# Normalising the last head group in the transposed layout: 0/1 selection matrices in column tiles instead of transposes, and one joint second variance

## Chip, cores and metric

One core of one Trainium2 chip runs the whole kernel. The metric is the device time of one execution in microseconds, the median of the runs. All data is float32 (the scores use float32r).

## What is computed

One transformer layer over 2048 tokens of 128 values, 16 heads of 8:

```python
def kernel_func(q, k):                      # attention weights without softmax
    scores = einsum('bhqd,bhkd->bhqk', q, k) / sqrt(HD)
    w = relu(scores)
    return w / (sum(w, axis=-1, keepdims=True) + 1e-6)
xn  = layernorm(x)
out = (kernel_func(q, k) @ v) @ w_out + b_out          # q, k, v from xn @ w_qkv
y   = xn + out
x1  = x + (y - mean(y)) * rsqrt(var(y) + 1e-5) * gamma + beta
h   = layernorm(x1)
x2  = x1 + sqrt((h @ cos(theta + theta_noise))**2 + (h @ sin(phi + phi_noise))**2)
```

## The kernel before

The engines' programs are written by hand, each with its own order of instructions; semaphores join them. The queries are cut into NC = 4 chunks of CW = 512 columns, the heads into G = 4 groups of HPG = 4. A pass takes one chunk through 4 x 16 steps: a step computes the scores of 128 keys for the four heads of a group in four row tiles of the array (`score_step`, L1119), ScalarE and VectorE share the relu (L603, L609, L781, L786), and `value_step` (L1154) multiplies by the values in four column tiles, one head in each 32 rows of a PSUM bank `pv`. The 32 rows of a head hold its 8 value rows, then at row HD = 8 the sum of the weights, then zeros. ScalarE copies the finished bank to `pv_sb`.

For passes 0 to 2 the normalisation goes through DRAM and is spread over the following pass: SyncE saves `pv_sb`, loads the sums and the values in other layouts, VectorE adds the epsilon and inverts (`invert_sums`), SyncE spreads the inverses, GpSimd multiplies (`scale_o`) into `oT` (heads x 8 rows, tokens along the columns), the stationary operand of the projection. The hooks in `after_pass` say at which step each engine does its part. The epsilon of each token is scaled by its standard deviation (`eps_std`); transposed, it lies in DRAM as `eps_dram`, from which four loads fill `eps_spread` at the end of pass 0.

The last chunk has no pass behind it. Its first three groups go the same way through DRAM during the last group (96 rows of `oT`). The last group, rows 96 to 128, is the tail, done in two halves of 256 tokens:

- ScalarE copies each half of `pv[1]` to `pv_sb` (L693).
- TensorE transposes it, tokens onto partitions (`transpose_pv`, L1161); VectorE adds the epsilon, inverts, multiplies (`normalise`, L796, L800, L801) into `o_sb`, whose other columns are zero; TensorE transposes back (`transpose_o`, L1161); ScalarE copies the 32 rows to `oT` (`take_oT`, L635).
- TensorE adds the projection to the residual in PSUM: `tail_x` (L1257) multiplies x_tail by the identity to start a bank, `project_tail` (L1267) adds the projection. Each half has two such banks: which = 0 for the statistics, which = 1, scaled by gamma, for x1.
- VectorE takes mean and variance (L950, L956), ScalarE the root (L696), VectorE inverts it (L962) and makes x1 (`tail_x1`, L969).
- TensorE transposes x1 (`transpose_x1`), ScalarE copies it (L644), TensorE multiplies by the centred cos and sin (`ffn`, L1212), ScalarE squares (L649), VectorE adds the squares (`tail_sum`, L979), ScalarE takes the root scaled by the second variance (`magnitude`, L659), VectorE adds x1 (`tail_finish`, L987), SyncE stores. The second variance comes from `post_stats` and `post_inverse` on x1 (L857 to L867), one half after the other.

Of the kernel before, what the change touches and what calls it, by code (L numbers as in the profile page):

```python
# [58 lines left out]
NORM_SEQ = 2  # L59
# [21 lines left out]
def block_kernel(nc, x, w_qkv, w_out, b_out, gamma, beta, theta, phi, theta_noise, phi_noise, out):  # L81
# [3 lines left out]
    with ctx:  # L85
        def sb(name, shape, dt=F32):
            return ctx.enter_context(nc.sbuf_tensor(name, shape, dt))

        def sem(name):
            return ctx.enter_context(nc.semaphore(name))  # L90
# [25 lines left out]
        den = sb("den", [P, TPC, HPG])  # L116
# [6 lines left out]
        o_sb = sb("o_sb", [P, TPC, D])  # L123
# [8 lines left out]
        turns = sb("turns", [P, 2, D])  # L132
        ffn_w = sb("ffn_w", [P, 2, D])
# [87 lines left out]
        pvT_done = sem("pvT_done")  # L221
# [8 lines left out]
        o_zero = sem("o_zero")  # L230
        norm_own = sem("norm_own")
        normed = sem("normed")

        oT_done = sem("oT_done")
# [32 lines left out]
        def chunk(c):  # L267
            return bass.ds(c * TPC, TPC)

        class Part:  # L270
# [3 lines left out]
            def __init__(self, j, half=None):  # L274
                self.j, self.half = j, half
                self.n = j if half is None else j + half
                self.lo, self.tiles = (0, TPC) if half is None else (2 * half, 2)
                self.own = (post_own[half or 0], POST_SEQ * (0 if half else j))
                if half is None:
                    self.o_bank = self.y_bank = pv[1]  # L280
                    self.x1_bank = pv[0]
                else:
                    self.pv_bank, self.o_bank = sc[half][:, 0, :], sc[half][:, 1, :]
                    self.y_bank = sc[2][:, half, :]
                    self.x1_bank = self.pv_bank
# [38 lines left out]
        with nc.Block() as block:  # L324

            @block.sync
            def _(sp):
# [103 lines left out]
            def _(pool):  # L431
# [41 lines left out]
                nc.gpsimd.memset(o_sb[:, :, 0:(G - 1) * HPG * HD], 0.0).then_inc(o_zero, 1)  # L473
# [61 lines left out]
                nc.gpsimd.memset(eps_col[:, :], LN_EPS).then_inc(eps_ready, 1)  # L535
                scale_o(0, G)
# [15 lines left out]
            def _(act):  # L552
# [79 lines left out]
                def take_oT(part):  # L632
                    last = slice((G - 1) * HPG * HD, P)
                    act.wait_ge(oT_done, part.half + 1)
                    nc.scalar.copy(oT[last, part.cols()],  # L635
                                   part.o_bank[last, 0:part.tiles * P]).then_inc(oT_ready, 1)

# [65 lines left out]
                for stage in (square, magnitude):  # L703
                    for part in halves:
                        stage(part, 0)
                        stage(part, 1)
# [3 lines left out]
            def _(dve):  # L710
# [78 lines left out]
                def normalise(half, bank, tiles):  # L789

                    own = Own(dve, norm_own, NORM_SEQ * half)
                    n = tiles.stop - tiles.start
                    pvT = bank[:, 0:n * P].rearrange("p (t i v) -> p t i v", t=n, i=HPG)
                    dve.wait_ge(pvT_done, half + 1)
                    first_tile = (NC - 1) * TPC
                    own(nc.vector.tensor_tensor(  # L796
                        den[:, tiles, :], pvT[:, :, :, HD],
                        eps_std[:, first_tile + tiles.start:first_tile + tiles.stop].unsqueeze(2).to_broadcast(
                            [P, n, HPG]), ALU.add))
                    own(nc.vector.reciprocal(den[:, tiles, :], den[:, tiles, :]))  # L800
                    nc.vector.tensor_tensor(  # L801
                        o_sb[:, tiles, (G - 1) * HPG * HD:].rearrange("p t (i d) -> p t i d", i=HPG),
                        pvT[:, :, :, 0:HD], den[:, tiles, :].unsqueeze(3).to_broadcast([P, n, HPG, HD]),
                        ALU.mult).then_inc(normed, 1)

                def invert_sums(c, groups):
# [6 lines left out]
                    dve.wait_ge(eps_loaded, 16 * NC)  # L813
# [174 lines left out]

                for part in halves:
                    normalise(part.half, part.pv_bank, part.sl())  # L990
# [3 lines left out]
                tail_stats(second)  # L994
                tail_inverse(first)
                tail_variance(second)
# [3 lines left out]
                for stage in (lambda p: post_stats(p, x1), lambda p: post_inverse(p, 1)):  # L1000
                    for part in halves:
                        stage(part)
                dve.wait_ge(x2_ready, NC - 1)
                for stage in (tail_sum, tail_finish):
                    for part in halves:
                        stage(part, 0)
                        stage(part, 1)
# [3 lines left out]
            def _(pe):  # L1011
# [152 lines left out]
                def transpose_pv(half, bank, tiles):  # L1164
                    pe.wait_ge(pv_out, G * NC + half)
                    transpose_tiles(bank, lambda t: pv_sb[:, t * P:(t + 1) * P], tiles, pvT_done)

                def transpose_o(part):
                    pe.wait_ge(o_zero, 1)
                    pe.wait_ge(normed, part.half + 1)  # L1170
                    transpose_tiles(part.o_bank, lambda t: o_sb[:, t, :], part.all(), oT_done)
# [99 lines left out]
                pe.wait_ge(tail_ready, 2)  # L1271
                tail_x(first, 1, pv[0])
                for part in halves:
# [37 lines left out]
```

## Time and profile before

| | |
|---|---|
| three runs | 421.67, 421.72, 548.05 us (median 421.72) |
| profiled execution | 422.16 us, of which the span from first to last instruction is 420.4 |
| busy: TensorE, VectorE, ScalarE, GpSimd | 98%, 79%, 81%, 12% of the span |
| granted TensorE clock | 1.00 in all of the span |
| last value matmul ends | 407.05 us after the span's start |

All times are from the start of the span. Busy shares are means over passes (TensorE always at work) and a tail (nobody is); the tail is read from the timelines.

### The profile page before, as it was taken

Reading aid. Unit: us, or ns where it says so; the run is one execution under the profiler, and the core shown is the slowest. Engines: PE = TensorE matmul, PEld = TensorE weight load, DVE = VectorE, ACT = ScalarE, POOL = GpSimd, SP = SyncE. Lnnn points to the kernel's source line nnn. Section 1 sums busy time; section 2 is a strip of 40 time slices with the busy share of each in tenths; the row PEclk is TensorE's granted clock in tenths of the full one; section 3 lists DMA queues with packets and bytes.
Section 4 is the critical chain, followed back from the end, with each engine's and each line's share of the span. In section 5 each row is a group of like instructions: output and inputs, shape, how many; then the busy total and the mean of one; then the engine's idle time right before and its main releaser. Section 6 shows DMA issues by size and latency. Waiting matters only on the chain.

```text
span 420.4 us, 8994 instructions
## 1 busy us (share of the span) xinstructions
PE 412.1 (98%) x3263; PEld 120.0 (29%) x3263; DVE 331.6 (79%) x654; ACT 341.1 (81%) x611; POOL 49.4 (12%) x57
## 2 busy tenths in 40 slices
PE   8899999999999999999999999999999999999995
PEld 6333222222222222222222322222222322222234
DVE  5877778888688897777778898777778798777856
ACT  3879888888788888888888888788887888888864
POOL 2004000099101000000401000000100100000111
PEclk9999999999999999999999999999999999999999
DMA  5117841010021100001011100101012000000200
GB/s 168 31 51 147 162 114 51 2 27 25 4 75 46 51 2 21 33 0 52 27 53 55 27 27 8 43 2 52 27 50 58 2 27 1 27 2 27 68 2 25
DMA packets 11741, 17.54 MB, mean 42 GB/s; under 512 B 3684, under 2 KB 5364, under 8 KB 11316
## 3 DMA queue, kind: packets, MB, share of 16 engines
q1 hardware_dynamic: 11556, 16.84, 15.0%
q8 instruction: 28, 0.46, 0.4%
q10 hardware_dynamic: 144, 0.13, 0.1%
q14 instruction: 13, 0.11, 0.1%
HBM read 3.99 MB, written 5.11 MB: 22 GB/s over the span
## 4 chain that ended last, share of the span: by engine, by line
PE 97%; DVE 2%; ACT 1%; issue 0%; POOL 0%; POOLq 0%; DVEq 0%
PE pv L1154 61%; PE sc L1119 27%; PE pv L1212 2%; PE pv L1054 1%; PE pv L1074 1%; PE pv L1066 1%; PE pv L1045 1%; PE pv L1180 1%; PE pv L1161 0%; PE pv L1034 0%; PE sc L1212 0%; PE sc L1081 0%; DVE x L969 0%; PE sc L1161 0%; PE sc L1267 0%
## 5 line engine op out<-in xcount | busy, mean ns | idle before, releaser
L1154 PE MATMUL pv<-w_buf,v_sb 128*32 128x512 f32 x2048 | 272.3, 604 | 0.0
L781 DVE TENSOR_SCALAR w_buf<-sc 128x512 f32<-128x512 f32 x256 | 176.9, 691 | 68.9 <-PE sc L1119 59.2
L603 ACT ACTIVATE w_buf<-sc 128x512 f32<-128x512 f32 x256 | 153.2, 598 | 62.8 <-PE sc L1119 61.5
L609 ACT ACTIVATE w_buf<-sc 128x512 f32<-128x512 f32 (+1 forms) x254 | 182.5, 719 | 0.0
L1119 PE MATMUL sc<-q_rep,k_rep 32*128 32x512 f32 x1024 | 133.2, 494 | 1.0 <-DVE w_buf L781 0.9
L786 DVE TENSOR_SCALAR w_buf<-sc 128x512 f32<-128x512 f32 x182 | 125.0, 687 | 0.0
L1119 PEld LDWEIGHTS sc<-q_rep,k_rep 32*128 32x128 f32 x1024 | 52.0, 181 | 215.0 <-ACT w_buf L603 176.5
L1154 PEld LDWEIGHTS pv<-w_buf,v_sb 128*32 128x32 f32 x2048 | 40.4, 108 | 66.5 <-ACT w_buf L609 35.4
L494 POOL TENSOR_TENSOR oT<-o_raw,o_scale 128x512 f32<-128x512 f32 (+1 forms) x4 | 5.1, 1281 | 88.4 <-issue 60.8
L510 POOL TENSOR_TENSOR mag<-sq 128x256 f32<-128x256 f32 x6 | 4.4, 731 | 77.5 <-ACT sq L649 77.5
L500 POOL TENSOR_TENSOR x<-x,mv 128x512 f32<-128x512 f32 (+1 forms) x5 | 4.3, 870 | 68.2 <-DVE x L883 55.7
L514 POOL TENSOR_TENSOR x<-x,mag 128x512 f32<-128x512 f32 x3 | 3.8, 1280 | 52.7 <-ACT mag L659 52.7
L453 POOL TENSOR_TENSOR xn<-x_sb,mv 128x512 f32<-128x512 f32 x4 | 4.2, 1043 | 42.8 <-issue 42.8
L444 POOL MEMSET v_sb<- 128x1472 f32 x4 | 5.2, 1326 | 31.6 <-DVE inv_var L736 31.6
L617 ACT COPY pv_sb<-pv 128x512 f32<-128x512 f32 x15 | 8.8, 586 | 0.1
L1212 PE MATMUL pv<-ffn_w,x1T 128*128 128x256 f32 x24 | 6.8, 405 | 0.0
L742 DVE TENSOR_TENSOR q_lo<-pv,q_hi 128x512 fp32r<-128x512 f32 x4 | 2.8, 692 | 4.0 <-ACT q_hi L568 4.0
L659 ACT ACTIVATE mag<-mag,iv_p 128x128 f32<-128x128 f32 x16 | 5.4, 398 | 0.0
L484 POOL TENSOR_TENSOR x_sb<-x_sb,beta_b 128x512 f32<-128x512 f32 x4 | 5.0, 1271 | 0.0
L1074 PE MATMUL pv<-ident 128*128 128x128 f32 x14 | 3.4, 432 | 1.5 <-POOL ident L434 1.5
L1212 PEld LDWEIGHTS pv<-ffn_w,x1T 128*128 128x128 f32 x24 | 4.1, 189 | 1.8 <-issue 1.5
L1045 PE MATMUL pv<-xT,w 128*128 128x512 f32 x8 | 4.4, 637 | 0.1
(132 smaller groups left out, 152.3 us busy)
## 6 DMA issues: line engine op xcount, KB each, us to landing
pv_dram<-pv_sb SPq DMA_DIRECT2D x15, 256.0 KB, 2.0
q_rep<-q_hi SPq DMA_DIRECT2D x30, 64.0 KB, 2.1
q_rep<-q_lo SPq DMA_DIRECT2D x30, 64.0 KB, 2.1
k_rep<-k_hi SPq DMA_DIRECT2D x6, 256.0 KB, 4.1
k_rep<-k_lo SPq DMA_DIRECT2D x6, 256.0 KB, 5.4
x_sb<-x_dram SPq DMA_DIRECT2D x3, 256.0 KB, 3.9
o_raw<-pv_dram SPq DMA_DIRECT2D x3, 256.0 KB
o_scale<-inverse_dram SPq DMA_DIRECT2D x3, 256.0 KB
```

The costliest lines, as they stand in the source:

```text
L444: nc.gpsimd.memset(v_sb[:, :, heads, HD + 1:VW], 0.0).then_inc(v_pad, 1)
L603: nc.scalar.activation(w_buf[:, s % W_STEPS, 0, :], early[:, 0, :], ACT.Relu).then_inc(relu[0], 2 if none else 1)
L609: nc.scalar.activation(w_buf[:, s % W_STEPS, 2:2 + n, :], late[:, 0:n, :], ACT.Relu).then_inc(relu[0], 1)
L617: nc.scalar.copy(pv_sb[:, :], bank[:, :]).then_inc(pv_out, 1)
L659: last = nc.scalar.activation(mag[:, t, :], mag[:, t, :], ACT.Sqrt, scale=iv_p[:, 1, t:t + 1])
L781: nc.vector.tensor_scalar(w_buf[:, s % W_STEPS, 1, :], early[:, 1, :], 0.0, None, ALU.max).then_inc(relu[1], 2 if both else 1)
L786: nc.vector.tensor_scalar(w_buf[:, s % W_STEPS, 2 + n:4, :], late[:, n:2, :], 0.0, None, ALU.max).then_inc(relu[1], 1)
L1045: nc.tensor.matmul(k_bank[c], w3[:, 1, :], xT[:, c * CW:(c + 1) * CW], start=True, stop=True).then_inc(k_done, 1)
L1074: nc.tensor.matmul(bank[:, 0:P], ident[:, :], ident[:, :], start=True, stop=True)
L1119: last = nc.tensor.matmul(sc[buf][:, i % 2, :], k_rep[rows, g, k * P:(k + 1) * P], q_rep[rows, g, :], start=True, stop=True)
L1154: last = nc.tensor.matmul(bank[32 * i:32 * i + 32, :], v_sb[:, k, HPG * g + i, :], w_buf[:, s % W_STEPS, i, :], start=(k == 0), stop=(k == ...
L1212: last = nc.tensor.matmul(bank[:, m * 2 * D:(m + 1) * 2 * D], x1T[:, t * P:(t + 1) * P], ffn_w[:, :, :].rearrange("p c d -> p (c d)"), sta ...
```

## The change

- The epsilons of the last chunk are loaded once more, by SyncE at the end of pass 0, as `eps_tail`: the row of 512 tokens on all 128 partitions.
- GpSimd makes two 128x32 matrices of zeros and ones from the identity (`select`, in the space of `turns`): `select[:, 0, :]` brings a head's sum row to the 8 rows of this head, `select[:, 1, :]` its 8 value rows to them.
- In place of the transposes TensorE runs `start_sums` (identity columns times `eps_tail` start the sum's rows of a bank with the epsilon) and `select_rows` (sums and values), each into 32 rows of a bank: one column tile.
- VectorE's `normalise` inverts 32 rows x 256 columns from PSUM into `o_scale`, and multiplies the values by it straight into `oT`. `o_sb`, `den`, `transpose_pv`, `transpose_o` and `take_oT` go.
- `tail_x(first, 1)` moves from in front of the tail to behind the second projection. The second half's `tail_variance` moves ahead of the first half's inverse.
- The second variance is made once for both halves (`x1_inverses`). ScalarE's squares and roots interleave.

```diff
+                            sp.dma_start(eps_tail[:, :], eps_dram[chunk(NC - 1), :].rearrange("t p -> (t p)")
+                                         .partition_broadcast(P)).then_inc(eps_loaded, 16)
...
-                nc.gpsimd.memset(o_sb[:, :, 0:(G - 1) * HPG * HD], 0.0).then_inc(o_zero, 1)
...
+                by_head = ident[:, :].rearrange("p (i v) -> p i v", i=HPG)
+                for n, columns in enumerate((by_head[:, :, HD:HD + 1].to_broadcast([P, HPG, HD]),
+                                             by_head[:, :, 0:HD])):
+                    nc.gpsimd.tensor_copy(select[:, n, :].rearrange("p (i d) -> p i d", i=HPG),
+                                          columns).then_inc(tail_ready, 1)
...
-                for stage in (take_oT, tail_root, take_x1T):
+                for stage in (tail_root, take_x1T):
                     for part in halves:
                         stage(part)
...
+                first, second = halves
+                square(first, 0)
+                square(first, 1)
+                square(second, 0)
+                magnitude(first, 0)
+                square(second, 1)
+                magnitude(first, 1)
+                magnitude(second, 0)
+                magnitude(second, 1)
...
+                def normalise(part):
+
+                    rows, cols = slice((G - 1) * HPG * HD, P), part.cols()
+                    dve.wait_ge(den_done, part.half + 1)
+                    if part.half == 0:
+                        dve.wait_ge(oT_ready, NC - 1)
+                    nc.vector.reciprocal(o_scale[rows, cols],
+                                         part.den_bank[part.den_rows, 0:part.tiles * P]).then_inc(den_inverse, 1)
+                    dve.wait_ge(den_inverse, part.half + 1)
+                    nc.vector.tensor_tensor(oT[rows, cols], part.o_bank[part.o_rows, 0:part.tiles * P],
+                                            o_scale[rows, cols], ALU.mult).then_inc(oT_ready, 1)
...
-                    dve.wait_ge(eps_loaded, 16 * NC)
+                    dve.wait_ge(eps_loaded, 16 * (NC + 1))
...
+                def x1_inverses():
+
+                    for t in range(TPC):
+                        last = nc.vector.bn_stats(stats_p[:, t, :], x1[:, t, :])
+                    own[1](last)
+                    for t in range(TPC):
+                        last = nc.vector.bn_aggr(mv_p[:, t, :], stats_p[:, t, :])
+                    own[1](last)
+                    own[1](nc.vector.tensor_scalar_add(iv_p[:, 1, :], mv_p[:, :, 1], LN_EPS))
+                    nc.vector.reciprocal(iv_p[:, 1, :], iv_p[:, 1, :]).then_inc(iv_ready[1], 2)
...
                 tail_stats(second)
+                tail_variance(second)
                 tail_inverse(first)
-                tail_variance(second)
...
+                def start_sums(part):
+
+                    nc.tensor.matmul(part.den_bank[part.den_rows, 0:part.tiles * P],
+                                     ident[:, part.den_rows], eps_tail[:, part.cols()],
+                                     start=True, stop=False)
+
+                def select_rows(part):
+
+                    pe.wait_ge(pv_out, G * NC + part.half)
+                    nc.tensor.matmul(part.den_bank[part.den_rows, 0:part.tiles * P], select[:, 0, :],
+                                     pv_sb[:, part.cols()], start=False, stop=True)
+                    nc.tensor.matmul(part.o_bank[part.o_rows, 0:part.tiles * P], select[:, 1, :],
+                                     pv_sb[:, part.cols()], start=True, stop=True).then_inc(den_done, 1)
...
-                pe.wait_ge(tail_ready, 2)
-                tail_x(first, 1, pv[0])
-                for part in halves:
-                    transpose_pv(part.half, part.pv_bank, part.all())
+                pe.wait_ge(tail_ready, 4)
+                pe.wait_ge(eps_loaded, 16 * (NC + 1))
+                start_sums(first)
+                start_sums(second)
+                select_rows(first)
+                select_rows(second)
                 tail_x(first, 0, first.y_bank)
-                transpose_o(first)
-                transpose_o(second)
                 project_tail(first, 0, first.y_bank, proj_done)
                 tail_x(second, 0, second.y_bank)
                 project_tail(second, 0, second.y_bank, proj_done)
+                tail_x(first, 1, pv[0])
                 project_tail(first, 1, pv[0], scaled_done)
```

## Rows read from the trace of the kernel before

**Rows 1.** The page: the span, and the chain that ended last, by engine.

```profile
span 420.4 us, 8994 instructions
...
PE 97%; DVE 2%; ACT 1%; issue 0%; POOL 0%; POOLq 0%; DVEq 0%
...
```

**Rows 2.** The chain from 407.05 us on, shares of the window by line.

```profile
...
by line: PE sc L1212 9.4%; DVE x L969 8.9%; PE sc L1161 8.3%; PE sc L1267 7.9%; DVE x L987 7.4%; DVE mag L979 6.0%; issue 4.6%; PE pv L1257 4.5%; DVE stats_p L950 3.6%; DVE o_sb L801 3.3%; PE sc L1257 3.1%; DVE den L800 3.1%; ACT sq L649 2.
...
```

**Rows 3.** Timeline of PE (TensorE), 404 to 417 us: start, us, what, count.

```profile
...
404.26 2.78 PE L1154 MATMUL pv<-w_buf,v_sb 128*32 128x512 f32 x24
...
407.54 0.71 PE L1161 MATMUL sc<-ident,pv_sb 128*128 128x128 f32 x4
...
410.80 0.61 PE L1267 MATMUL sc<-wout_tail,oT 128*128 128x128 f32 x4
411.24 0.61 PE L1267 MATMUL pv<-wout_tail,oT 128*128 128x128 f32 x4
...
414.10 1.89 PE L1212 MATMUL sc<-ffn_w,x1T 128*128 128x256 f32 x8
```

**Rows 4.** Timeline of ACT (ScalarE), 407 to 419 us.

```profile
...
407.11 0.65 ACT L693 COPY pv_sb<-pv 128x256 f32<-128x256 f32 x2 [1.23 <-PE pv L1154]
...
409.91 0.36 ACT L635 COPY oT<-sc 32x256 f32<-32x256 f32 x1 [0.15 <-PE sc L1161]
...
414.73 1.68 ACT L649 ACTIVATE sq<-sc 128x256 f32<-128x256 f32 x4
416.37 1.28 ACT L659 ACTIVATE mag<-mag,iv_p 128x128 f32<-128x128 f32 x4
```

**Rows 5.** Timeline of DVE (VectorE), 406 to 420 us.

```profile
...
408.08 0.17 DVE L796 TENSOR_TENSOR den<-sc,eps_std 128x8 f32<-128x8 f32 x1 [2.95 <-PE sc L1161]
...
409.09 0.23 DVE L801 TENSOR_TENSOR o_sb<-sc,den 128x64 f32<-128x64 f32 x1
410.56 0.50 DVE L950 BATCH_NORM_STATS2 stats_p<-sc 128x6 f32<-128x128 f32 x2 [1.24 <-PE sc L1267]
411.09 0.25 DVE L956 BATCH_NORM_AGGREGATE mv_p<-stats_p 128x2 f32<-128x6 f32 x2
411.44 0.50 DVE L950 BATCH_NORM_STATS2 stats_p<-sc 128x6 f32<-128x128 f32 x2
...
412.06 0.23 DVE L956 BATCH_NORM_AGGREGATE mv_p<-stats_p 128x2 f32<-128x6 f32 x2
...
413.16 0.61 DVE L969 SCALAR_TENSOR_TENSOR x<-pv,rs_p,x_sb 128x128 f32<-128x128 f32 x2
413.80 1.01 DVE L857 BATCH_NORM_STATS2 stats_p<-x 128x6 f32<-128x128 f32 x4
...
415.98 0.90 DVE L979 TENSOR_TENSOR mag<-sq 128x128 f32<-128x128 f32 x4
...
```

**Rows 6.** Timeline of SyncE's queue, 114 to 136 us.

```profile
...
115.64 2.54 SPq L414 DMA_DIRECT2D eps_spread<-eps_dram  x4
...
```

**Rows 7.** Waits of that queue, 105 to 135 us: total, times, longest.

```profile
...
SPq L370 <- DVE inverse L815: 4.4, 1, 4.4
...
```

**Rows 8.** Timeline of POOL (GpSimd), 100 to 136 us.

```profile
...
133.94 1.28 POOL L494 TENSOR_TENSOR oT<-o_raw,o_scale 128x512 f32<-128x512 f32 x1 [27.62 <-DMA o_scale<-inverse_dram]
```

**Rows 9.** Groups on VectorE, shapes apart: busy us, mean ns of one.

```profile
...
L815 DVE RECIPROCAL inverse<-sums 128x64 f32<-128x64 f32 x3 | 1.7, 553 | 0.1
...
L867 DVE RECIPROCAL iv_p<-iv_p 128x4 f32<-128x4 f32 x6 | 1.1, 178 | 0.2
...
L815 DVE RECIPROCAL inverse<-sums 96x64 f32<-96x64 f32 x1 | 0.5, 548 | 0.0
...
L800 DVE RECIPROCAL den<-den 128x8 f32<-128x8 f32 x2 | 0.4, 204 | 0.1
L895 DVE TENSOR_TENSOR ffn_w<-ffn_w,pv 128x256 f32<-128x256 f32 x1 | 0.4, 399 | 0.0
...
```

**Rows 10.** Windows of PE: stretch, length, busy (count), granted clock, DMA.

```profile
...
1.50:3.00 1.50, 1.48 (x7) 1.00 0.58 107
409.80:413.80 4.00, 3.37 (x23) 1.00 0.00 0
...
```

More of the change, by code:

```diff
@@ L58 @@
 PI_BELOW = 3.1415925
-NORM_SEQ = 2
 POST_SEQ = 7
@@ L122, in block_kernel @@
         inverse_dram = nc.dram_tensor("inverse_dram", [H, CW], F32).ap()
-        o_sb = sb("o_sb", [P, TPC, D])
+        eps_tail = sb("eps_tail", [P, CW])
         oT = sb("oT", [P, CW])
@@ L132, in block_kernel @@
         turns = sb("turns", [P, 2, D])
+        select = turns[:, :, 0:VW]
         ffn_w = sb("ffn_w", [P, 2, D])
@@ L229, in block_kernel @@
         oT_three = sem("oT_three")
[L230 to L234, printed above, removed]
+        den_inverse = sem("den_inverse")
+        den_done = sem("den_done")
         oT_ready = sem("oT_ready")
@@ L279, in __init__ @@
                 if half is None:
-                    self.o_bank = self.y_bank = pv[1]
+                    self.y_bank = pv[1]
                     self.x1_bank = pv[0]
                 else:
-                    self.pv_bank, self.o_bank = sc[half][:, 0, :], sc[half][:, 1, :]
+                    self.den_bank, self.o_bank = sc[half][:, 0, :], sc[half][:, 1, :]
+                    self.den_rows, self.o_rows = ((slice(64, 96), slice(96, 128)),
+                                                  (slice(0, 32), slice(32, 64)))[half]
                     self.y_bank = sc[2][:, half, :]
-                    self.x1_bank = self.pv_bank
+                    self.x1_bank = self.den_bank
             def sl(self):
@@ L630, in sqrt_table @@
                     nc.scalar.activation(spare_act[:, :], rstd[:, 0:1], ACT.Sqrt)
[L632 to L636, printed above, removed]
                 def post_root(part):
@@ L699, in _ @@
                 act.wait_ge(eps_ready, 1)
-                for stage in (take_oT, tail_root, take_x1T):
+                for stage in (tail_root, take_x1T):
                     for part in halves:
                         stage(part)
-                for stage in (square, magnitude):
-                    for part in halves:
-                        stage(part, 0)
-                        stage(part, 1)
+                first, second = halves
[7 more added lines that the diff above has]
+                magnitude(second, 1)
             @block.vector
@@ L787, in relu_step @@
                                                 0.0, None, ALU.max).then_inc(relu[1], 1)
[L789 to L804, printed above, removed]
+                def normalise(part):
[8 more added lines that the diff above has]
+                                            o_scale[rows, cols], ALU.mult).then_inc(oT_ready, 1)
                 def invert_sums(c, groups):
@@ L987, in tail_finish @@
                     nc.vector.tensor_tensor(x2[:, t, :], x2[:, t, :], mag[:, t, :], ALU.add).then_inc(x2_ready, 1)
+                def x1_inverses():
[7 more added lines that the diff above has]
+                    nc.vector.reciprocal(iv_p[:, 1, :], iv_p[:, 1, :]).then_inc(iv_ready[1], 2)
                 for part in halves:
-                    normalise(part.half, part.pv_bank, part.sl())
+                    normalise(part)
                 first, second = halves
@@ L999, in _ @@
                 tail_x1(second)
-                for stage in (lambda p: post_stats(p, x1), lambda p: post_inverse(p, 1)):
-                    for part in halves:
-                        stage(part)
+                x1_inverses()
                 dve.wait_ge(x2_ready, NC - 1)
[L1004 to L1007, printed above, removed]
+                for part in halves:
+                    tail_sum(part, 0)
+                    tail_sum(part, 1)
+                for part in halves:
+                    tail_finish(part, 0)
+                    tail_finish(part, 1)
             @block.tensor
@@ L1162, in transpose_tiles @@
                     last.then_inc(done, 1)
[L1164 to L1171, printed above, removed]
+                def start_sums(part):
[8 more added lines that the diff above has]
+                                     pv_sb[:, part.cols()], start=True, stop=True).then_inc(den_done, 1)
                 def project_out(part):
@@ L1269, in project_tail @@
                     last.then_inc(done, 1)
-                pe.wait_ge(tail_ready, 2)
-                tail_x(first, 1, pv[0])
-                for part in halves:
-                    transpose_pv(part.half, part.pv_bank, part.all())
+                pe.wait_ge(tail_ready, 4)
[4 more added lines that the diff above has]
+                select_rows(second)
                 tail_x(first, 0, first.y_bank)
-                transpose_o(first)
-                transpose_o(second)
                 project_tail(first, 0, first.y_bank, proj_done)
```

2 lines of the change are left out of this document (removed).

## The prediction, made before the changed kernel was built

> **What bounds the kernel now.** I read the page first: its span, and the chain that ended last [rows 1]. TensorE holds 97% of that chain, so over some 407 us nothing but matmuls counts; VectorE and ScalarE appear on it only at the end. The chain of the last 13.4 us alone, by line [rows 2], looks different: no group has 10% of it, and projection, statistics, x1, transposes, feed-forward, sums and the final addition take turns. Behind the last value matmul the work is one serial relay between three engines, and whoever holds the baton sets the end. So I read that stretch as a timeline of each engine [rows 3 to 5] and looked, at each hand-over, for what came last.
>
> The relay before. The values end at 407.05; ScalarE takes the first half of them at 407.11 [rows 4]; TensorE transposes from 407.54 [rows 3]; VectorE begins on the sums at 408.08 and has finished both halves by 409.3 (six operations of 8 and 64 elements a partition) [rows 5]. Then come two transposes back and two copies, the second of them 409.91 to 410.27 [rows 4]; the first projection lets VectorE start its statistics at 410.56 [rows 5]; the second starts at 410.80 [rows 3]; x1 of the second half ends at 413.77 (413.16 and 0.61) [rows 5]; its transposes are issued ahead of the feed-forward, which follows at 414.10 [rows 3], and the squares start at 414.73 [rows 4]. From there ScalarE is busy without a gap, 1.68 us of squares and 1.28 us of roots.
>
> **Part 1: everything ahead of the tail.** SyncE's queue gets one more transfer of 256 KB behind the four of the epsilons. Issuing one of those took 2.54 / 4 = 0.64 us [rows 6], so the save of the values and the loads behind it start 0.6 us later. The same queue later waits 4.4 us for the inverses [rows 7], which VectorE makes at a fixed step of its own order; 0.6 us vanishes in that wait. Without it, pass 1's projection would be late by that much, once. VectorE's wait for this transfer stands behind its wait for the sums, which the same queue issues later. On GpSimd a memset goes and two copies of 32 columns come, in front of an idle stretch of 27.6 us, where even 512 columns take only 1.28 us [rows 8]. TensorE's wait for four tail_ready instead of two, and VectorE's for oT_ready, are for things done long before. Sum: nothing; at most 0.6.
>
> **Part 2: from the values to VectorE.** Out go the scaled x_tail product (put later) and four transposes; in come two start_sums and four selections with 256 moving columns in column tiles. How fast are column tiles here? The 24 value records of 512 columns took 2.78 us, 0.116 us each, while the eight feed-forward records of 256 columns on the whole array took 1.89, one each 0.22 (the last lasts 0.38) [rows 3]. So four tiles side by side do 3.7 times the work, and I take two tiles to run side by side as well: the first half's four records (a product is two) in 4 x 0.108 + 0.16 = 0.59 us. The start_sums fill 0.43 us from 407.05 on, about until the first copy is there; the selection starts at 407.52 and VectorE at 408.20 (0.09 behind the last of its matmuls, as before: two of the four transposes take 0.45 of the 0.54 us from 407.54 to 408.08), against 408.08 [rows 5]: **+0.1**. Bounds: -0.1 if it drains no later than transposes; +0.9 if the tiles don't overlap (twice 0.43).
>
> **Part 3: the division.** This is where I expect the change to lose. Before, tokens lay on the partitions, so a reciprocal had 8 elements a partition. Now tokens lie along the columns, and the sum has been copied to each of 32 rows: a reciprocal has 256 elements a partition, whatever the number of rows. Its price is in the trace at three widths: 178 ns for 4 elements, 204 for 8, 553 for 64 [rows 9], so (553 - 204) / 56 = 6.2 ns an element, against about 0.9 for an elementwise operation (0.23 us at 64 [rows 5], 0.40 at 256 [rows 9]). 96 rows cost 548 where 128 cost 553, so fewer rows don't help [rows 9]. That gives 204 + 248 x 6.23 = **1.75 us** for each of the two. No row has this operation with 256 elements or from PSUM; the bounds are 0.40 us, if it ran like the 256-column operation, and 2.2 us, four times the 64-element row, its fixed part included. I take 1.75, since three rows of the same instruction lie on one line (4 to 8 elements give 6.5 ns each).
> The Trainium skill (VectorE: DVE Perf Modes, Walkthrough: the 8-slice pipeline in each mode) says that the reciprocal is an iterated division with a repeat count of 8. Read as eight cycles of its 0.96 GHz an element, that would be 2.1 us for 256 and 0.8 us more in the sum; the rows give six cycles, and I stay with them.
>
> The timeline, with 0.03 us between dependent operations: reciprocal 408.20 to 409.95, multiplication (0.40) to 410.39, reciprocal to 412.16, multiplication to 412.60. This writes oT directly, so two transposes back and two ScalarE copies go. The first projection can start at 410.43, the second at 412.64 instead of 410.80: +1.8. VectorE, which does both halves before any statistics, starts these at 412.63 instead of 410.56: **+2.07**. In the old kernel the division cost VectorE 1.24 us, in the new one 4.40; what the removed transposes and copies give back is 409.32 to 410.56, 1.24 us. The difference, 3.16 - 1.24 = 1.92, and the 0.12 of part 2 are the same sum in other terms.
>
> **Part 4: statistics and x1.** Before, 3.21 us from the first statistics to the end of x1 (410.56 to 413.77). The second half's statistics waited 0.10 us for their projection (411.34 to 411.44 [rows 5]); that goes, since they now come at 413.4 and the projection is done at about 413.3. The second half's aggregation (0.23 [rows 5]) used to sit in the wait for the first half's root and reciprocal; it is now ahead of them: +0.2. Net **+0.1**, and x1 ends at 415.96. The first half's scaled product is now queued behind the second projection: 412.64, then 0.44 each for the projection, the x_tail product and the product itself, done at 414.1 [rows 3]; x1 of the first half asks for it at about 414.4. Cover 0.3 us; if it went, x1 would be late by the remainder.
>
> **Part 5: joint variance and the new order.** The two chains took VectorE 2.18 us (413.80 to 415.98 [rows 5]); the joint one saves two memsets, an addition and a reciprocal, about 0.3. It was hidden before: ScalarE had squares to do until 416.4 [rows 4]. Now the first root is wanted after three squares, 0.42 us earlier. Squares start at 414.73 + 2.19 = 416.92 and three end at 418.18; VectorE is through its chain at 417.9 and the first sum at 418.15. It just fits. ScalarE's eight operations stay the same and gapless, so the end moves with the first square: **+-0** (-0.1 to +0.2). The final additions and the last store move with it.
>
> **Sum.** 0.12 + 1.95 + 0.12 = +2.2 us. The profiled execution took 422.16 us (420.4 span), so it becomes 424.4 (span 422.6). The median of the runs is 0.44 lower: 421.72 + 2.2 = **423.9 us**, 0.5% slower and far inside the 2% that count here as no change. Of the three runs one took 548; I leave it out.
>
> **Rivals.**
> *The reciprocal is cheap here.* If it has the price of any 256-column operation (0.40), VectorE finishes the division at 408.20 + 4 x 0.43 = 409.9, the second projection starts at 409.95, statistics at 409.9 instead of 410.56, x1 ends at 413.2: -0.6, **421.1 us**, not slower. That is the change as its removals suggest it: two hops fewer. It decides below about 0.65 us a reciprocal (1.75 - 2.2 / 2). For it: there is no row at this width or from PSUM. Against it: three widths of one instruction on one line of slope.
> *TensorE's clock falls in the holes.* TensorE now has nothing from about 408.7 to 410.4 and from 411.4 to 412.6. At the low level the same columns take twice as long: 7 matmuls of 128 columns in 1.5 us in the first stretch of the kernel, 0.21 each [rows 10], against four in 0.44 here [rows 3]. The column of the granted clock says 1.00 in both [rows 10], so it is the spacing that tells, and it fits 1.2 and 2.4 GHz. If it fell at about 412, the five groups from the second projection on would take 0.88 instead of 0.44, x1 of the second half would come 1.9 later, transposes and first feed-forward 0.65, the other three 1.3: 3.8 more, **427.7 us**; only from the feed-forward on, 1.9 more, 425.8. Against it: the holes are short and matmuls stand between them. The Trainium skill (TensorE: Matmul & The Clock Gate, Part 1: The HAM clock gate) has such a rule, that the array's clock is halved after idleness; no stretch of this trace shows it in mid-kernel.
> *The tiles don't overlap*, so the column tiles don't do what they are for: +0.9 in part 2, **424.7 us**. Against it the value matmuls of every step.
>
> **Chances.** The sum as forecast, 423.2 to 424.6: 0.76. Cheap reciprocal, 421.1: 0.08. Clock, 425.3 to 427.7: 0.08. Tiles, 424.7: 0.04. Something unseen: 0.04. The range of 8 in 10 takes in the forecast, the tiles and the bounds of parts 1 to 5 short of a cheap reciprocal: 422.8 to 425.3. Over 2% means 8.4 us: a tail of 13 us would have to grow by two thirds, which not even the clock does. Faster 0.01, same 0.98, slower 0.01.
>
> **What would show it.** In the profile after: two reciprocals of 32x256 with 1.75 us each, the second multiplication ending near 412.6; no oT copy on ScalarE; the second projection 1.8 us later; VectorE with about a third of the chain's last 15 us; matmul spacings as before. Wrong if the reciprocals are shorter than 1 us, if VectorE waits for the selections beyond 408.5, if matmul spacing in the tail has doubled, or if a gap stands between ScalarE's squares and roots.

## The result, and the profile after

The changed kernel takes 424.75 us in the median of 5 executions (424.23 to 425.18), the kernel before 421.93: a ratio of 1.007, 95% interval 1.0058 to 1.0082. One of the five executions of the kernel before took 548.05 us and is left out of the ratio. That is a little slower, and no change by the 2% that count here. Forecast were 423.9 us and a range of 422.8 to 425.3. The profiled execution took 425.18 us.

The page of it: span, granted clock in 40 slices, and the group that is new on VectorE (busy us, mean ns of one, idle before).

```profile
span 423.4 us, 8995 instructions
...
PEclk9999999999999999999999999999999999999987
...
L798 DVE RECIPROCAL o_scale<-sc 32x256 f32<-32x256 f32 x2 | 3.5, 1754 | 3.2 <-PE sc L1184 3.1
...
```

The two reciprocals cost 1754 ns each, as summed. But the last two slices of the clock read 8 and 7, where the kernel before had 1.00 throughout. TensorE's timeline, then its windows (stretch, length, busy, count, granted clock):

```profile
...
402.85 2.78 PE L1163 MATMUL pv<-w_buf,v_sb 128*32 128x512 f32 x24
...
409.12 0.71 PE L1281 MATMUL sc<-wout_tail,oT 128*128 128x128 f32 x4 [1.47 <-DVE oT L801]
...
411.36 1.22 PE L1281 MATMUL sc<-wout_tail,oT 128*128 128x128 f32 x4 [1.09 <-DVE oT L801]
412.38 1.06 PE L1271 MATMUL pv<-x_tail,ident 128*128 128x256 f32 x2
413.23 1.06 PE L1281 MATMUL pv<-wout_tail,oT 128*128 128x128 f32 x4
...
416.70 0.69 PE L1170 MATMUL sc<-ident,x 128*128 128x128 f32 x2 [0.28 <-DVE x L967]
417.18 2.00 PE L1226 MATMUL sc<-ffn_w,x1T 128*128 128x256 f32 x8
```

```profile
...
409.00:410.00 1.00, 0.88 (x6) 1.00 0.00 0
410.00:411.00 1.00, 0.27 (x2) 0.78 0.00 0
411.00:412.00 1.00, 0.64 (x3) 0.50 0.00 0
...
417.00:418.00 1.00, 1.00 (x6) 0.81 0.00 0
...
```

The values end at 402.85 + 2.78 = 405.63. Behind the selections and one x_tail product TensorE waits 1.47 us for the first projection at 409.12, and 1.09 more for the second at 411.36. In between the granted clock falls to 0.50, about 410.6, which is 0.3 us into the second wait, and is back at about 417.4. From 412.38 on each group of four records of 128 columns, or two of 256, takes 0.85 us to the next (412.38 to 413.23) where it took 0.44 before [rows 3]. VectorE's timeline:

```profile
...
406.85 1.76 DVE L798 RECIPROCAL o_scale<-sc 32x256 f32<-32x256 f32 x1 [3.14 <-PE sc L1184]
408.64 0.43 DVE L801 TENSOR_TENSOR oT<-sc,o_scale 32x256 f32<-32x256 f32 x1
409.10 1.75 DVE L798 RECIPROCAL o_scale<-sc 32x256 f32<-32x256 f32 x1
410.88 0.42 DVE L801 TENSOR_TENSOR oT<-sc,o_scale 32x256 f32<-32x256 f32 x1
411.34 0.49 DVE L948 BATCH_NORM_STATS2 stats_p<-sc 128x6 f32<-128x128 f32 x2
...
412.62 0.49 DVE L948 BATCH_NORM_STATS2 stats_p<-sc 128x6 f32<-128x128 f32 x2 [0.51 <-PE sc L1281]
...
414.33 0.61 DVE L967 SCALAR_TENSOR_TENSOR x<-pv,rs_p,x_sb 128x128 f32<-128x128 f32 x2 [0.88 <-PE pv L1281]
...
416.03 0.61 DVE L967 SCALAR_TENSOR_TENSOR x<-pv,rs_p,x_sb 128x128 f32<-128x128 f32 x2 [0.90 <-PE pv L1281]
...
```

Read it as in [rows 5]. The division starts 1.22 us behind the values (1.03 before) and keeps VectorE until 411.30; the statistics start at 411.34. Then come waits that the kernel before hardly had: 0.51 for the second projection, 0.88 and 0.90 for the two scaled products. x1 ends at 416.64. ScalarE follows:

```profile
...
417.92 1.25 ACT L647 ACTIVATE sq<-sc 128x256 f32<-128x256 f32 x3
...
```

The squares start 1.28 us behind the end of x1; before it was 0.96 [rows 4, 5]: the transposes and the first feed-forward product are still slow.

Measured from the last value matmul, the tail has grown from 13.35 us (407.05 to 420.4) to 17.77 (405.63 to 423.4), by 4.4 and not by 2.2. The span grew by 3.0 only, since all that lies ahead was 1.4 us shorter in this execution. The experiments separate the two.

### The profile page after: what moved, and what is told of

It is laid out like the page before. It is cut to its first block, busy times and chain, and to the rows that moved or that the text cites. A ratio compares the mean times of both kernels' runs of the same rounds, so it can differ in the third digit from the quotient of the medians.

```text
span 423.4 us, 8995 instructions
## 1 busy us (share of the span) xinstructions
PE 413.4 (98%) x3267; PEld 120.7 (28%) x3267; DVE 334.3 (79%) x648; ACT 340.2 (80%) x609; POOL 49.4 (12%) x58
## 4 chain that ended last, share of the span: by engine, by line
PE 96%; DVE 2%; ACT 1%; issue 0%; POOL 0%; POOLq 0%; DVEq 0%
PE pv L1163 60%; PE sc L1128 27%; PE pv L1226 2%; PE pv L1063 1%; DVE o_scale L798 1%; PE pv L1075 1%; PE pv L1054 1%; PE pv L1194 1%; PE pv L1083 1%; PE pv L1170 0%; PE pv L1281 0%; PE pv L1271 0%; PE sc L1281 0%; PE pv L1031 0%; PE pv L1043 0%
## 5 line engine op out<-in xcount | busy, mean ns | idle before, releaser
L798 DVE RECIPROCAL o_scale<-sc 32x256 f32<-32x256 f32 x2 | 3.5, 1754 | 3.2 <-PE sc L1184 3.1
```

The costliest lines, as they stand in the source:

```text
L798: nc.vector.reciprocal(o_scale[rows, cols], part.den_bank[part.den_rows, 0:part.tiles * P]).then_inc(den_inverse, 1)
```

## The experiments

Ratios are against the kernel before, run beside them: 421.93 us beside the kernel after, 421.88 beside e1 to e4, 421.38 beside e5 to e8. So kernels of different sets are compared by their ratios and tails. "Tail" is the span behind the last value matmul in the profiled execution.

| kernel | median us | ratio, 95% interval | tail us |
|---|---|---|---|
| before | 421.93 / 421.88 / 421.38 in the three sets | | 13.35 |
| after | 424.75 | 1.007 (1.0058 to 1.0082) | 17.77 |
| e1_copy | 421.06 | 0.9988 (0.9979 to 0.9997) | 12.71 |
| e2_filler | 423.36 | 1.0044 (1.0032 to 1.0056) | 15.42 |
| e3_joint | 421.82 | 0.9999 (0.9990 to 1.0008) | 13.37 |
| e4_early_x | 423.47 | 1.0052 (1.0034 to 1.0070) | 15.35 |
| e5_spread | 422.52 | 1.0020 (1.0011 to 1.0029) | 14.13 |
| e6_delay | 426.63 | 1.0117 (1.0103 to 1.0131) | 17.95 |
| e7_again | 425.10, one execution | | 16.91 |
| e8_best | 421.08 | 0.9992 (0.9982 to 1.0002) | 12.98 |

### e1_copy: is it the reciprocals?

```diff
-                    nc.vector.reciprocal(o_scale[rows, cols],
-                                         part.den_bank[part.den_rows, 0:part.tiles * P]).then_inc(den_inverse, 1)
+                    nc.vector.tensor_copy(o_scale[rows, cols],
+                                          part.den_bank[part.den_rows, 0:part.tiles * P]).then_inc(den_inverse, 1)
```

> The changed kernel with VectorE's two 32x256 reciprocals of the tail replaced by copies (the last head group is multiplied by its sum instead of divided by it). Theory: the two reciprocals (1.75 us each) are the loss, and the holes they leave on TensorE are what let its granted clock fall to 0.50 between 410.4 and 417.2 us. A 256-column copy takes about 0.40, so the division ends 2.7 us earlier, the holes shrink below those of the kernel before, the clock stays at 1.00 and no x1 waits for its scaled product: 12.8 us from the last value matmul to the end of the span instead of 17.8, and 421.3 us. Rival, the clock falls for another reason (the column tiles, the order of the products): 2.7 us gained and no more, 15 us of tail, 422.0 us, and a granted clock below 1.00 in it.

This kernel leaves out the division of the last head group, so its output isn't that of the layer; it serves for the time alone.

VectorE's timeline:

```profile
...
408.11 0.42 DVE L798 COPY o_scale<-sc 32x256 f32<-32x256 f32 x1 [3.14 <-PE sc L1184]
...
409.94 0.49 DVE L948 BATCH_NORM_STATS2 stats_p<-sc 128x6 f32<-128x128 f32 x2
...
```

The copies take 0.42, the division 1.8 us instead of 4.5, the tail 12.71, and the clock stays at 1.00 in it. Without the price of the reciprocals the change would be what its removals promise: the tail is 0.6 us shorter than before, the time 0.5 by the ratio and 0.8 by the medians (forecast for a cheap reciprocal: 0.6). The rival's 422.0 is out: no execution took more than 421.39.

### e2_filler: is the clock a cause, or only a companion?

```diff
                 tail_x(first, 0, first.y_bank)
+                warm_up(6, pv[0])
                 project_tail(first, 0, first.y_bank, proj_done)
                 tail_x(second, 0, second.y_bank)
+                warm_up(4, pv[0])
                 project_tail(second, 0, second.y_bank, proj_done)
```

> The changed kernel with ten matmuls of the identity by itself put into TensorE's two holes (six before the first projection, four before the second, into a bank that is started anew later). Theory: the holes bring the clock down, and the low clock is what makes x1 wait 0.88 and 0.90 us for the scaled products and the second statistics 0.51 us. With the holes filled the granted clock stays at 1.00, these waits go, the tail takes 15.6 instead of 17.8 us, as I forecast without a fall of the clock, and the time is 424.1 less what the runs of the kernel after already had of it, 423 to 424. Rival, the waits come from the queue order (the x_tail product moved behind the second projection), whatever the clock: the waits stay and the time is that of the changed kernel, 424.7.

TensorE's timeline, with the first filler and the second projection, and VectorE's:

```profile
...
403.30 2.78 PE L1163 MATMUL pv<-w_buf,v_sb 128*32 128x512 f32 x24
...
407.94 1.50 PE L1083 MATMUL pv<-ident 128*128 128x128 f32 x12
...
411.81 0.71 PE L1281 MATMUL sc<-wout_tail,oT 128*128 128x128 f32 x4 [0.20 <-DVE oT L801]
...
```

```profile
...
407.30 1.76 DVE L798 RECIPROCAL o_scale<-sc 32x256 f32<-32x256 f32 x1 [3.14 <-PE sc L1184]
...
411.79 0.49 DVE L948 BATCH_NORM_STATS2 stats_p<-sc 128x6 f32<-128x128 f32 x2
...
413.49 0.61 DVE L967 SCALAR_TENSOR_TENSOR x<-pv,rs_p,x_sb 128x128 f32<-128x128 f32 x2
...
414.40 0.61 DVE L967 SCALAR_TENSOR_TENSOR x<-pv,rs_p,x_sb 128x128 f32<-128x128 f32 x2
...
```

Ten matmuls whose results nobody reads make the kernel 1.4 us faster in the median (1.1 by the ratios) and its tail 2.35 shorter in the profiled execution. The mean clock was 1.00 in all five executions. Nothing waits any more: the second statistics follow the first, and x1 its inverse. The order of the queue is that of the kernel after, so the waits were the clock's. This is also the clean view of the other terms, used below.

### e4_early_x: the same with real work

```diff
                 tail_x(first, 0, first.y_bank)
+                tail_x(second, 0, second.y_bank)
+                tail_x(first, 1, pv[0])
+                tail_x(second, 1, pv[1])
                 project_tail(first, 0, first.y_bank, proj_done)
-                tail_x(second, 0, second.y_bank)
                 project_tail(second, 0, second.y_bank, proj_done)
-                tail_x(first, 1, pv[0])
                 project_tail(first, 1, pv[0], scaled_done)
-                tail_x(second, 1, pv[1])
                 project_tail(second, 1, pv[1], scaled_done)
```

> The changed kernel with all four x_tail products ahead of the first projection, in TensorE's first hole: 1.3 us of real work there, and only projections left behind the division. Theory: at either clock level the four projections (0.44 us each, 0.88 at the low level) are through before VectorE asks for them, x1 waits for nothing, and 2.2 us of the changed kernel's tail go, 15.6 us of tail, 423 to 424 us, even if the granted clock still falls in the second hole, where nothing is put. Rival, only a clock that stays high brings the time back: the clock falls in the second hole, transposes and feed-forward run at half speed, and under 1 us is gained, 424 us or more.

TensorE's timeline, the first and the second projection:

```profile
...
409.84 0.71 PE L1281 MATMUL sc<-wout_tail,oT 128*128 128x128 f32 x4 [0.18 <-DVE oT L801]
412.08 0.71 PE L1281 MATMUL sc<-wout_tail,oT 128*128 128x128 f32 x4 [1.53 <-DVE oT L801]
...
```

The tail is 15.35 us as in e2_filler. I had expected the clock to fall in the second hole, 1.53 us of waiting at 412.08 (before it, nothing since 410.55). In the profiled execution it didn't, so this profile can't say what the order is worth at the low level. Of the six executions four had a mean clock of 1.000 (423.01 to 423.52 us), one 0.996 (424.25) and one 0.992 (425.25). One filled hole makes the fall rarer and doesn't exclude it; those two executions are about as slow as the kernel after (424.23 to 425.18). That the clock fell in them is read from their means, since they have no timeline.

### e3_joint: parts 4 and 5 alone, on the kernel before

```diff
                 tail_stats(second)
+                tail_variance(second)
                 tail_inverse(first)
-                tail_variance(second)
...
-                for stage in (lambda p: post_stats(p, x1), lambda p: post_inverse(p, 1)):
-                    for part in halves:
-                        stage(part)
+                x1_inverses()
```

Squares and roots are in the order of the kernel after.

> The kernel before with only parts 4 and 5 of the change: the second half's aggregation ahead of the first half's inverse, one joint second variance, squares and roots interleaved; transposes and the small reciprocals stay. Theory: ScalarE's eight operations from the first square on set the end and nothing ahead of them moves by more than 0.1 us, so the time is that of the kernel before within 0.2 us. Rival, the joint variance is worth its 0.3 us of VectorE: 0.3 us faster.

ScalarE's timeline, squares and roots:

```profile
...
414.85 1.25 ACT L649 ACTIVATE sq<-sc 128x256 f32<-128x256 f32 x3
...
416.57 0.98 ACT L659 ACTIVATE mag<-mag,iv_p 128x128 f32<-128x128 f32 x3
```

No difference: 0.9999. x1 ended 0.1 us later (the aggregation), and from the first square to the last root it took 2.70 us instead of 2.92 [rows 4], so 0.2 came from interleaving. Both as small as said, of opposite sign.

### e5_spread: the price goes with the elements of a partition

```diff
-                    nc.vector.reciprocal(o_scale[rows, cols],
-                                         part.den_bank[part.den_rows, 0:part.tiles * P]).then_inc(den_inverse, 1)
+                    nc.vector.reciprocal(inverse_tail[:, part.half, :],
+                                         part.den_bank[:, 0:64]).then_inc(den_inverse, 1)
...
+                    for n in range(4):
+                        last = nc.vector.tensor_tensor(
+                            oT[rows, part.lo * P + 64 * n:part.lo * P + 64 * n + 64],
+                            part.o_bank[part.o_rows, 64 * n:64 * n + 64],
+                            inverse_tail[32 * n:32 * n + 32, part.half, :], ALU.mult)
...
```

Not shown: the sums are started and selected in four pieces of 64 columns, one for each column tile, and the x_tail products stand as in e4_early_x, which is what this kernel is compared with.

> The changed kernel with the x_tail products ahead (as in e4_early_x), and with the sums of a half selected into all four column tiles, 64 tokens in each: one reciprocal of 128x64 a half in place of 32x256, and four multiplications of 32x64 in place of one of 32x256. Theory: a reciprocal costs 6.2 ns an element of a partition whatever the rows, so it falls from 1.75 to 0.55 us; the four multiplications take 0.22 each, 0.9 at most. A half then costs VectorE 1.5 instead of 2.2 us, both 1.4 less: 14.0 us from the last value matmul to the end of the span instead of the 15.35 of e4_early_x, and about 422.2 us. Rival, the price goes with the operation and not with the columns (its division unit shared between rows): the 128-row reciprocal costs as much as before, 1.7 us or more, and the time is 424 us.

VectorE's timeline, the division:

```profile
...
408.30 0.56 DVE L799 RECIPROCAL turns<-sc 128x64 f32<-128x64 f32 x1 [3.26 <-PE sc L1192]
408.90 0.96 DVE L803 TENSOR_TENSOR oT<-sc,turns 32x64 f32<-32x64 f32 x4
409.89 0.56 DVE L799 RECIPROCAL turns<-sc 128x64 f32<-128x64 f32 x1
...
411.43 0.50 DVE L953 BATCH_NORM_STATS2 stats_p<-sc 128x6 f32<-128x128 f32 x2
...
```

Each column tile holds 64 tokens. The same 8192 inverses of a half, on four times the rows: 0.56 instead of 1.75 us. The four multiplications take 0.24 each, one behind the other. 1.2 us of tail come back against e4_early_x (forecast 1.4), and the kernel is still 0.2% slower than before: its division is 3.1 us (408.30 to 411.43), and before, with the transposes and copies, it was 2.5.

### e6_delay: the same idle time in the kernel before

```diff
                     own(nc.vector.reciprocal(den[:, tiles, :], den[:, tiles, :]))
+                    dve.wait_ge(oT_ready, NC - 1)
+                    own(nc.vector.reciprocal(o_scale[(G - 1) * HPG * HD:, 0:2 * P],
+                                             wqkv_sb[(G - 1) * HPG * HD:, 0:2 * P]))
```

> The kernel before with one more reciprocal of 32x256 in each half's division, of numbers that nobody reads, between the small reciprocal and the multiplication. Transposes, copies, the order of the products and both second variances are as before. Theory: it is VectorE's 1.75 us a half that costs the time and that opens the holes on TensorE; this kernel then loses 3.5 us in its tail (16.9 instead of 13.35), and the granted clock may fall in the holes and cost up to 2.4 more: 425.4 to 427.8 us, by the profile 3.5 us plus whatever stretch shows 0.50. Rival, the column tiles or the moved x_tail product are needed for the fall and for half of the loss: part of the 3.5 us is absorbed in waits that the old order has, and under 2.5 us is lost, below 424.4.

TensorE's timeline, and windows:

```profile
...
404.07 2.78 PE L1157 MATMUL pv<-w_buf,v_sb 128*32 128x512 f32 x24
...
410.48 0.41 PE L1164 MATMUL sc<-ident,o_sb 128*128 128x128 f32 x2 [1.99 <-DVE o_sb L804]
412.83 0.43 PE L1164 MATMUL sc<-ident,o_sb 128*128 128x128 f32 x2 [1.94 <-DVE o_sb L804]
...
```

```profile
...
413.00:414.00 1.00, 1.00 (x7) 0.54 0.00 0
...
```

The tail grows by 4.6 us, the 3.5 of the two reciprocals and 1.1 more, most of it 0.93 us in which the second statistics wait for their projection. There are no column tiles and no moved product behind the values here, and the clock falls all the same, at about 413, behind two waits of 2 us. So holes that VectorE's delay opens are enough. (Its mean clock was 0.992 to 0.994 in four executions.)

### e7_again: where does it fall?

> The changed kernel, unaltered, looked at once more for where in the tail the granted clock falls. Theory: what the fall costs depends on where it begins and ends; the mean clock of the other executions (0.995 against 0.992 in the profiled one) says that 4 us instead of 7 were granted at 0.50. I expect a low stretch again between 409 and 418 us, and a tail of 15.4 us plus the waits for the products in that stretch, up to 17.8. Rival, the fall is an accident of the one execution: 1.00 throughout, 15.4 us of tail.

The windows at the edges of the low stretch:

```profile
...
412.00:413.00 1.00, 0.88 (x4) 0.55 0.00 0
...
415.00:416.00 1.00, 1.00 (x7) 0.75 0.00 0
...
```

And VectorE's two waits for the scaled products:

```profile
...
415.09 0.61 DVE L967 SCALAR_TENSOR_TENSOR x<-pv,rs_p,x_sb 128x128 f32<-128x128 f32 x2 [0.88 <-PE pv L1281]
...
416.25 0.61 DVE L967 SCALAR_TENSOR_TENSOR x<-pv,rs_p,x_sb 128x128 f32<-128x128 f32 x2 [0.35 <-PE pv L1281]
...
```

Low from about 412.1 to 415.5, half as long as in the first profile: the waits for the scaled products are 0.88 and 0.35 us instead of 0.88 and 0.90, the tail is 16.91. It is not an accident: of the kernel after, all six executions that I have show a mean clock of 0.995 or less.

The head of the kernel explains the rest. The same matmul of 384 columns (two records), in the kernel after and in e1_copy:

```profile
...
4.96 0.81 PE L1090 MATMUL sc<-wqkv_sb,x1T 128*128 128x384 f32 x2
...
```

```profile
...
5.51 1.49 PE L1090 MATMUL sc<-wqkv_sb,x1T 128*128 128x384 f32 x2
...
```

In the first microseconds matmuls run at half speed though the row of the granted clock says 1.00 [rows 10], until the clock rises at a time that differs from execution to execution. It rose early in the profiled execution of the kernel after, late in those of e1_copy, before and e3_joint, and that is the 1.3 to 1.4 us by which the values end sooner (405.63 against 406.89 to 407.05). The start of the first score matmul shows it, in the kernel after and in the kernel before:

```profile
...
9.27 0.51 PE L1128 MATMUL sc<-q_rep,k_rep 32*128 32x512 f32 x4 [0.17 <-DVE k_rep L757]
...
```

```profile
...
10.62 0.51 PE L1119 MATMUL sc<-q_rep,k_rep 32*128 32x512 f32 x4 [0.17 <-DVE k_rep L754]
```

From there to the start of the last group of value matmuls (402.85 and 404.26) it is 393.6 us in both, so all of the difference arises in the first ten microseconds. It isn't the change's: in e7_again, the same program as the kernel after, the same matmul starts at 10.01. The 44 executions of the kernel before in the two sets sort the same way: mean clock 1.000 421.95 to 422.13 us (14 of them), 0.999 421.07 to 421.94 (20), 0.998 420.81 to 421.14 (10). A lower mean goes with a shorter time. In e8_best, whose profiled execution has 0.998, the fall is at about 417.5, behind the last matmul at 414.5, where it costs nothing. The kernel before is finished with TensorE when the clock falls, the kernel after isn't. That rise and fall hang together, both early or both late, is my reading of these few profiles and isn't shown; the fastest execution of e5_spread (421.61 us) has a mean of 1.000, so a short time and a low mean don't always go together.

### e8_best: what can be kept

```diff
                 tail_x(first, 0, first.y_bank)
+                tail_x(second, 0, second.y_bank)
                 transpose_o(first)
                 transpose_o(second)
                 project_tail(first, 0, first.y_bank, proj_done)
-                tail_x(second, 0, second.y_bank)
```

The rest is e3_joint without the move of `tail_variance(second)`.

> The kernel before with what the runs so far make cheap: transposes and small reciprocals kept, joint second variance, squares and roots interleaved, the second half's aggregation left where it was, and the second half's x_tail product moved ahead of the transposes back, into a stretch where TensorE waits for VectorE. Theory: interleaving gained 0.2 us between first square and last root in e3_joint, and the aggregation lost 0.1 there; the early product lets the second projection start at 410.3 instead of 410.8, of which VectorE can use 0.1. So 0.3 us faster than before, 421.6 us, 13.05 us of tail. Rival, TensorE's product delays the first transpose back by what it wins: no difference.

TensorE's timeline:

```profile
...
402.94 2.78 PE L1170 MATMUL pv<-w_buf,v_sb 128*32 128x512 f32 x24
...
406.76 1.03 PE L1273 MATMUL sc<-x_tail,ident 128*128 128x256 f32 x4
...
408.52 1.19 PE L1283 MATMUL sc<-wout_tail,oT 128*128 128x128 f32 x8
...
```

The eight projection records now follow each other, the tail is 12.98 us (forecast 13.05), and the median is 0.3 below the kernel before. By the interval it can't be told from no change. At the same mean clock of 1.000 its executions take 421.70 to 421.74 us and those of before 421.96 to 422.08.

## Why the prediction was right, and where it wasn't

The terms, with e2_filler as the execution in which the clock stayed (from its rows above; before from [rows 3 to 5]):

| step | forecast | measured |
|---|---|---|
| 2: values to VectorE (1.03 us before) | +0.12 | 1.22: +0.19 |
| 3: division to first statistics (2.48) | +1.95 | 407.30 to 411.79: +2.01 |
| 4: statistics to x1 (3.21) | +0.12 | 411.79 to 415.01: +0.01 |
| 5: x1 to the end (6.63) | 0 | 415.01 to 421.5: -0.14 |
| sum | +2.2 | +2.07 |
| clock (a rival, 0.08) | 0 | +2.35 in the profiled execution, +1.5 in e7_again |

In the median the time grew by 2.8 us, 0.7 more than the 2.1 of the terms. I read that remainder as what the low clock costs, less what shorter heads give back: the values ended 1.4 us (kernel after), 0.7 (e7_again) and 1.0 (e2_filler) sooner than in the profiled execution of the kernel before. By the ratios of the executions the kernel with filled holes loses 1.9 us (1.0044) and the kernel after 2.9 (1.007), so on average the fall costs about 1.1 us.

**Part 3** was right in mechanism and in size: 1.754 for 1.75. The slope from three narrower rows held at four times their width, from PSUM and on 32 rows. The Trainium skill's repeat count of 8 (VectorE: DVE Perf Modes, Walkthrough: the 8-slice pipeline in each mode), read as eight cycles an element, would have given an estimate of 2.1; the measurement decides for six.

**Part 2** was right: two column tiles do run side by side. In the timeline of e2_filler the records of sums and values start 0.01 us apart (406.57 and 406.58, 406.81 and 406.82), and all eight are over 0.9 us after the first has started. e1_copy, with the same selections, starts its first operation as late behind the values (1.22 us).

**Parts 4 and 5** were right in being small. The cover that I put at 0.3 us for the scaled product was enough in e2_filler, where x1 waits for nothing, and was gone at the low clock. Of the 2.35 us beyond e2_filler the kernel after loses 2.08 between the first statistics and the end of x1 (411.34 to 416.64 against 411.79 to 415.01), and 0.27 behind it.

**The clock, a rival,** is the step that failed: the sum held nothing for it. I gave it 0.08, because "the holes are short and matmuls stand between them"; the holes came out as foreseen (1.47 and 1.09 us where I had 1.7 and 1.2), and the clock fell in every execution of the kernel after. The sign that I had named for being wrong, a doubled spacing of the matmuls in the tail, is there, while the signs of part 3 came true. The rival's mechanism was as described, the x1 waits first: x1 of the second half came 2.1 us later than with a clock that stays, and I had said 1.9. Its price for the total (425.8 to 427.7) was too high: I had transposes and feed-forward 1.95 us slower in all, but the clock came back before the feed-forward's second product and they cost 0.27, and the heads were shorter.

The median, 424.75, lies inside the range between forecast and rival, 0.85 above the forecast value alone, and that is partly luck: with the start of the kernel before's profiled execution, the two profiled executions of the kernel after would have taken 426.6 and 425.8 us (an estimate: 425.18 + 1.42 and 425.10 + 0.66), both above 425.3. The Trainium skill (TensorE: Matmul & The Clock Gate, Part 1: The HAM clock gate) has the rule that idleness halves the clock; these runs agree with it (0.50 with holes of 1 to 2 us and little work between), and I should have given it about an even chance.

**Part 1** was right in its sum; its size came out in one profile and not in the others. Waits of SyncE's queue in the kernel after:

```profile
...
SPq L361 <- DMA pv_dram<-pv_sb: 3.7, 1, 3.7
SPq L368 <- DVE inverse L813: 1.9, 1, 1.9
...
```

The kernel after waits 3.7 us for the save of the values, where the kernel before waited 1.8, and the wait for the inverses has shrunk from 4.4 [rows 7] to 1.9: 2.5 us of delay, not 0.6, hidden all the same. In e2_filler, which has the same transfer, the same two waits are 1.7 and 3.7 us: 0.7 of delay, as forecast. The other four profiles with the transfer of 256 KB show 3.0 to 3.9 us of waiting for the save, the other three without it 1.7. So the transfer can delay the save, and doesn't always; what decides is open.

## What to carry to other kernels

Before turning an operation's layout, price every instruction in the new shape by its slope per element of a partition: a reciprocal costs here 6.2 ns for each, seven times an elementwise operation, so eight elements on 128 rows are cheap and 256 on 32 rows are not. A delay on another engine can also cost TensorE its clock: when a change opens holes of a microsecond or two in its queue, look for work that is ready (start products, identity products) and put it there; with one hole filled the clock still fell in two of six executions here, with both in none of five. And compare stages from a mark inside the kernel, not total times, where the start varies by more than the change is worth.

## What the runs showed that I had not expected

- One and the same program is granted different clocks: 0.50 for 6.8 us (410.6 to 417.4) in one execution of the kernel after and for 3.4 us in another; in e4_early_x, by the mean clock, a fall in two of six executions and none in four.
- In the first microseconds (up to 4.5 in the kernel after, up to 7.6 in the kernel before) matmuls run at half speed while the granted clock is recorded as 1.00 (1.49 us against 0.81 for the same product); only the spacing shows it. It moves the whole kernel by up to 1.4 us.
- With one more transfer of 256 KB ahead of a save the queue waited 3.0 to 3.9 us for the save in five profiles and 1.7 in a sixth; without it 1.7 to 1.8 in four.
- Four multiplications of 32x64 between different groups of 32 rows take 0.24 us each, 0.96 for four, without overlap, while four aggregations in one layout take 0.38 together.
